# Normalisation, splitting and rounding of eleven routing tiles moved from the router into the readout

## The reference

```python
x = x + tanh(g_xattn[0]) * readout(layernorm(x), ctx_2048, mask)   # softmax(x ctx^T / sqrt(512)) ctx
x = x + tanh(g_ffn[0]) * ffn(layernorm(x), router_w, wg, wu, wd)
...
logits = einsum('bsh,eh->bse', x, router_w)         # 8 experts
idx = argmax(logits, -1)
xq = clip(round(x * s), -128, 127) / s, s = 127 / max|x|   # each row, before each expert's ternary matrix
```

## Time and profile before

| what | us |
|---|---|
| median of 3 runs | 1711.72 |
| lowest, highest | 1705.13, 1719.22 |
| the profiled execution, its own time | 1718.61 |
| its span | 1716.9 |
| TensorE busy in the span | 1453.8 (85%) |
| VectorE busy | 1252.0 (73%) |
| ScalarE busy | 970.3 (57%) |
| GpSimd busy | 418.7 (24%) |

### The profile page before, as it was taken

One profiled execution on the slowest core, in us unless ns is written; L12 is line 12 of the kernel. 1 busy time (PEld: TensorE's weight loads), 2 busy tenths in 40 slices (PEclk: granted clock), 3 DMA queues, 4 the chain that ended last, 5 costly groups with the idle time before them and its releaser, 6 DMA issues. The chain is left out here.

```text
span 1716.9 us, 24336 instructions
## 1 busy us (share of the span) xinstructions
PE 1453.8 (85%) x8479; PEld 835.5 (49%) x8551; DVE 1252.0 (73%) x1525; ACT 970.3 (57%) x1440; POOL 418.7 (24%) x328
## 2 busy tenths in 40 slices
PE   4998996999822795779999999999968599999996
PEld 3454443555422443314555555555533466666663
DVE  4787855655484696669999999999787676665651
ACT  5787733344243684415766677676833676665651
POOL 0122200000053006204555656555740000000000
PEclk9999998999955896868999999999989799999998
DMA  6788760000064439310423324244254586666640
GB/s 226 220 271 296 236 210 26 0 0 0 1 243 167 141 119 228 88 49 15 103 71 88 83 68 107 70 102 132 73 167 178 181 291 216 220 213 224 225 144 25
DMA packets 145824, 236.74 MB, mean 138 GB/s; under 512 B 11324, under 2 KB 61503, under 8 KB 144584
## 3 DMA queue, kind: packets, MB, share of 16 engines
q1 hardware_dynamic: 140232, 210.39, 39.8%
q0 software_dynamic: 5504, 25.20, 4.0%
HBM read 169.48 MB, written 59.59 MB: 133 GB/s over the span
## 5 line engine op out<-in xcount | busy, mean ns | idle before, releaser
L1687 ACT ACTIVATE t_e<-t_psE 128x512 f32<-128x512 f32 x512 | 304.6, 597 | 139.6 <-PE t_psE L1812 131.3
L1725 DVE TENSOR_REDUCE t_nmax<-t_psM 128x1 f32<-128x1024 f32 x256 | 301.7, 1211 | 15.1 <-PE t_psM L1793 15.1
L1644 POOL TENSOR_TENSOR t_low<-t_e 128x1024 bf16<-128x1024 f32 x128 | 249.9, 1954 | 201.2 <-ACT t_e L1687 179.4
L1823 PE MATMUL t_psO<-t_e,vst 128*96 128x512 bf16 x512 | 201.1, 393 | 2.5 <-POOL t_low L1644 2.5
L1812 PE MATMUL t_psE<-qst,kst 99*128 99x512 bf16 x512 | 195.9, 384 | 0.1
L1823 PE MATMUL t_psO<-t_low,vst 128*96 128x512 bf16 x512 | 193.6, 378 | 0.0
L1793 PE MATMUL t_psM<-kst,qst 96*128 96x512 bf16 x512 | 165.1, 406 | 30.8 <-DVE t_nmax L1725 25.5
L1733 DVE TENSOR_TENSOR t_low<-t_e 128x1024 bf16<-128x1024 f32 x128 | 175.4, 1371 | 17.8 <-ACT t_e L1687 17.3
L2281 PE MATMUL e_psG<-prebob,e_w1p 128*128 (+1 forms) x1536 | 174.4, 277 | 11.6 <-DVE e_hT L2225 6.9
L2281 PEld LDWEIGHTS e_psG<-prebob,e_w1p 128*128 128x128 bf16 x1536 | 152.2, 99 | 34.1 <-issue 8.1
L2296 PE MATMUL e_psO<-e_w2p,e_hT 128*128 128x512 bf16 x752 | 164.9, 379 | 0.8
(11 more groups left out here) (235 smaller groups left out, 2286.5 us busy)
## 6 DMA issues: line engine op xcount, KB each, us to landing
piece<-in_L_ffn_w SPq DMA_DIRECT2D x32, 1024.0 KB, 13.9
xres<-in_L_ffn_w SPq DMA_DIRECT2D x32, 1024.0 KB, 14.6
wT<-ternary POOLq DMA_DIRECT2D x8, 1536.0 KB, 21.4
kst<-keys SPq DMA_DIRECT2D x96, 128.0 KB, 4.6
mixed<-t_ost SPq DMA_DIRECT2D x64, 192.0 KB
c_rows<-in_ctx SPq DMA_DIRECT2D x8, 1024.0 KB, 10.4
xres<-in_L_ffn_wg SPq DMA_DIRECT2D x8, 1024.0 KB, 7.8
xres<-in_L_ffn_wu SPq DMA_DIRECT2D x8, 1024.0 KB, 7.5
```

Source lines behind the costliest of these rows:

```text
L1644: nc.gpsimd.tensor_tensor(low[:, slot(h, u), :, :], e32[:, slot(h, u), :, :], upper(h, u), ALU.subtract).then_inc(lo_pool, 1)
L1687: nc.scalar.activation(e32[:, slot(h, u), i, :], psE[:, i, :], ACT.Exp, scale=SC).then_inc(expd, 1)
L1725: nc.vector.tensor_reduce(nmax[:, h // G % 2, h % G, u:u + 1], banks_of(place_of_max(b, m)).rearrange("p a t -> p (a t)"), AX_X, ALU.max, ...
L1823: last = nc.tensor.matmul(psO[0:VW, h % 2, :], vst[:, g, 2 * u + i, :].rearrange("p (w h) -> p h w", h=G)[:, h % G, :], part[:, i, :], sta ...
```

## The change

Tiles 0 to 10 (ROUTED_EARLY = 11) are normalised, split and rounded in the readout, by a function `route(r)` at the end of step r + 5 on VectorE and ScalarE. The router does this only for tiles 11 to 15 and transposes the others as they are. So that results can stay where they are written, the memory of the later stages (`late_flat`) is reserved from the start, and the first 22 of the 32 tiles of `ctxN` lie in it; `route` writes its pairs and integers over rows of `ctxN` whose batch is done, and uses rows of `ctxT` of the first batch as scratch. bn_aggr of a tile follows its bn_stats directly, GpSimd computes rstd for three batches within the readout (`rrstd`), and the hardware loops of the readout are written straight out on all engines. The second array `disp_late` holds the integers of the last two tiles, whose scales need an instruction of their own. On TensorE x_transposes(0) moves ahead of the router weights' transposes, and on ScalarE the copy of tile 0 ahead of the router weights' copy.

```diff
 # readout, ScalarE
+                def route(r):
+                    act.wait_ge(rnormed, r + 1)
+                    act.wait_ge(readout, r // QD * QD + 6)
+                    nc.scalar.copy(xpairs[:, r, 0, :], rxn[r % 2]).then_inc(rhi_done, 1)
+                    act.wait_ge(rq_ready, r + 1)
+                    nc.scalar.activation(disp[:, r, 0:D], rq32, ACT.Copy, bias=-MAGIC).then_inc(rq_cast, 1)
...
                     if further_x:
                         x_copy(t + 3, 1 - par)
+                    if 0 <= t - 5 < ROUTED_EARLY:
+                        route(t - 5)
...
-                with act.Fori(0, NT // 2 - 2) as i:
-                    step(2 * i, 0, 2, True)
-                    step(2 * i + 1, 1, 2, True)
+                for t in range(NT - 4):
+                    step(t, t % 2, 2, True)
 # readout, VectorE
                     nc.vector.bn_stats(stats[:, bass.ds(t, 1), :].rearrange("p o d -> p (o d)"), row).then_inc(stats_ready, 1)
+                    dve.wait_ge(stats_ready, t + 1)
+                    nc.vector.bn_aggr(moments[:, t, :], stats[:, t, :]).then_inc(moments_ready, 1)
+
+                def route(r):
+                    v, xn_r = nc.vector, rxn[r % 2]
+                    dve.wait_ge(rrstd_ready, r // QD + 1)
+                    if r >= 2:
+                        dve.wait_ge(rlo_done, r - 1)
+                    v.tensor_scalar(xn_r, xres[:, r, :], moments[:, r, 0:1], rrstd[:, r:r + 1],
+                                    ALU.subtract, ALU.mult).then_inc(rnormed, 1)
+                    dve.wait_ge(rnormed, r + 1)
+                    v.tensor_reduce(peak[:, r:r + 1], xn_r, AX_X, ALU.max, apply_absolute_value=True).then_inc(peaked, 1)
+                    dve.wait_ge(peaked, r + 1)
+                    v.tensor_scalar(amax[:, r:r + 1], peak[:, r:r + 1], EPS, 1.0 / 127.0, ALU.max, ALU.mult).then_inc(amax_ready, 1)
+                    dve.wait_ge(amax_ready, r + 1)
+                    v.reciprocal(invs[:, r:r + 1], amax[:, r:r + 1]).then_inc(invs_ready, 1)
+                    dve.wait_ge(invs_ready, r + 1)
+                    if r >= 1:
+                        dve.wait_ge(rq_cast, r)
+                    v.tensor_scalar(rq32, xn_r, invs[:, r:r + 1], MAGIC, ALU.mult, ALU.add).then_inc(rq_ready, 1)
+                    dve.wait_ge(rhi_done, r + 1)
+                    v.tensor_tensor(xpairs[:, r, 1, :], xn_r, xpairs[:, r, 0, :], ALU.subtract).then_inc(rlo_done, 1)
...
                         p_lo(t + 1, 1 - par)
+                    if 0 <= t - 5 < ROUTED_EARLY:
+                        route(t - 5)
...
-                dve.wait_ge(stats_ready, NT)
-                for t in range(NT):
-                    nc.vector.bn_aggr(moments[:, t, :], stats[:, t, :]).then_inc(moments_ready, 1)
 # router, ScalarE
-                for t in range(QD):
-                    high(t)
                 act.wait_ge(router_loaded, 16)
                 nc.scalar.copy(rpair[:, 0, :], rows[:, :]).then_inc(router_hi, 1)
+                x_copy(0)
                 act.wait_ge(router_xposed, 1)
                 nc.scalar.copy(rT[:, :, :], psR[:, :, 0:E]).then_inc(router_ready, 1)
-                for t in range(NT):
+                for t in range(1, NT):
                     x_copy(t)
-                    if t + QD < NT:
-                        high(t + QD)
-                    integers(t)
+                    if t - 1 + ROUTED_EARLY < NT:
+                        high(t - 1 + ROUTED_EARLY)
+                        integers(t - 1 + ROUTED_EARLY)
 # router, VectorE (route(t) here: normalise, peak, scale, reciprocal, multiply of one tile)
+                dve.wait_ge(consts, RSTD)
+                for t in range(ROUTED_EARLY, NT):
+                    route(t)
+                    if t > ROUTED_EARLY:
+                        low(t - 1)
+                low(NT - 1)
 # router, TensorE
                 def x_transposes(t):
-                    pe.wait_ge(x_lo, t + 1)
+                    if t >= ROUTED_EARLY:
+                        pe.wait_ge(x_lo, t - ROUTED_EARLY + 1)
```

More of the change, by code:

```diff
@@ L396, in _, with routed_views, readout_phase @@
                         gemm(q, n)
-def readout_phase(nc, sem, mask, gates, ident, ctxN, ctxT, xres, moments):
+ROUTED_EARLY, ROUTED_SHARED = 11, 14
+RW = 2 * D + DW
+def routed_views(flat):
+    v = flat[:, 0:ROUTED_SHARED * RW].rearrange("p (t w) -> p t w", w=RW)
+    return v[:, :, 0:2 * D].rearrange("p t (r d) -> p t r d", r=2), v[:, :, 2 * D:]
+def readout_phase(nc, sem, mask, gates, ident, ctxN, ctxT, xres, moments, amax, routed):
     SC = float(D) ** -0.5
@@ L459, in _ @@
                 nc.gpsimd.tensor_tensor(rstd[:, :], veps[:, :], half[:, :], ALU.pow).then_inc(rstd_ready, 1)
+                for b in range(B - 1):
+                    q = slice(b * QD, (b + 1) * QD)
+                    pool.wait_ge(moments_ready, (b + 1) * QD)
+                    nc.gpsimd.tensor_scalar(rveps[:, q], moments[:, q, 1], EPS, None, ALU.add).then_inc(rveps_ready, 1)
+                    pool.wait_ge(rveps_ready, b + 1)
+                    nc.gpsimd.tensor_tensor(rrstd[:, q], rveps[:, q], half[:, q], ALU.pow).then_inc(rrstd_ready, 1)
             @block.scalar
@@ L590, in _ @@
                 step(0, 0, False, True, True)
-                step(1, 1, True, True, True)
-                with dve.Fori(1, NT // 2 - 2) as i:
-                    step(2 * i, 0, True, True, True)
-                    step(2 * i + 1, 1, True, True, True)
+                for t in range(1, NT - 4):
+                    step(t, t % 2, True, True, True)
                 step(NT - 4, 0, True, False, True)
@@ L661, in _ @@
                 scores(1, 1, 0)
-                with pe.Fori(0, NT // 2 - 2) as i:
-                    step(2 * i, 0, True, True)
-                    step(2 * i + 1, 1, True, True)
+                for t in range(NT - 4):
+                    step(t, t % 2, True, True)
                 step(NT - 4, 0, True, True)
@@ L757, in _ @@
                     done(nc.gpsimd.memset(z, 0.0))
-                done(nc.gpsimd.memset(disp[:, :, D + 2:DW], 0.0))
+                done(nc.gpsimd.memset(disps[:, :, D + 2:DW], 0.0))
+                done(nc.gpsimd.memset(disp_late[:, :, D + 2:DW], 0.0))
                 for e in range(E):
@@ L815, in _ @@
                 v = nc.vector
-                def normalise(t):
-                    if t >= 2 * QD:
-                        dve.wait_ge(q_ready, t - 2 * QD + 1)
-                    v.tensor_scalar(xn[:, t % (2 * QD), :], xres[:, t, :], moments[:, t, 0:1], rstd[:, t:t + 1],
-                                    ALU.subtract, ALU.mult).then_inc(normed, 1)
-                def scale(g):
-                    for t in range(g * QD, (g + 1) * QD):
-                        dve.wait_ge(normed, t + 1)
-                        v.tensor_reduce(peak[:, t:t + 1], xn[:, t % (2 * QD), :], AX_X, ALU.max, apply_absolute_value=True).then_inc(amax_raw, 1)
-                    q = slice(g * QD, (g + 1) * QD)
-                    dve.wait_ge(amax_raw, (g + 1) * QD)
-                    v.tensor_scalar(amax[:, q], peak[:, q], EPS, 1.0 / 127.0, ALU.max, ALU.mult).then_inc(amax_ready, 1)
-                    dve.wait_ge(amax_ready, g + 1)
-                    v.reciprocal(invs[:, q], amax[:, q]).then_inc(invs_ready, 1)
@@ L843, in _, with route @@
-                dve.wait_ge(consts, RSTD)
-                for t in range(QD):
-                    normalise(t)
+                def route(t):
+                    n = t - ROUTED_EARLY
+                    if n >= 3:
+                        dve.wait_ge(x_lo, n - 2)
+                        dve.wait_ge(q_ready, n - 2)
+                    v.tensor_scalar(xn[:, t % 3, :], xres[:, t, :], moments[:, t, 0:1], rstd[:, t:t + 1],
+                                    ALU.subtract, ALU.mult).then_inc(normed, 1)
+                    dve.wait_ge(normed, n + 1)
+                    v.tensor_reduce(peak[:, t:t + 1], xn[:, t % 3, :], AX_X, ALU.max, apply_absolute_value=True).then_inc(amax_raw, 1)
+                    dve.wait_ge(amax_raw, n + 1)
+                    v.tensor_scalar(amax[:, t:t + 1], peak[:, t:t + 1], EPS, 1.0 / 127.0, ALU.max, ALU.mult).then_inc(amax_ready, 1)
+                    dve.wait_ge(amax_ready, n + 1)
+                    v.reciprocal(invs[:, t:t + 1], amax[:, t:t + 1]).then_inc(invs_ready, 1)
+                    dve.wait_ge(invs_ready, n + 1)
+                    if n >= 2:
+                        dve.wait_ge(q_cast, n - 1)
+                    v.tensor_scalar(q32[:, t % 2, :], xn[:, t % 3, :], invs[:, t:t + 1], MAGIC, ALU.mult, ALU.add).then_inc(q_ready, 1)
```

110 lines of the change are left out of this document (59 added, 51 removed).

## The result

| | before | changed |
|---|---|---|
| median of 14 runs, us | 1710.20 | 1700.02 |
| lowest, highest | 1705.13, 1719.22 | 1694.53, 1701.76 |
| profiled execution, own time (span) | 1718.61 (1716.9) | 1700.02 (1698.3) |

The ratio is 0.9929, 95% interval 0.9916 to 0.9942: 12.1 us faster, which is also the distance of the two means; the medians of the table lie 10.2 us apart. The forecast was 12.2. A second measurement beside other runs of the kernel before gave 0.9946 (0.9926 to 0.9967), 9.2 us, so the two together say 9 to 12.

What follows compares the result with a forecast made beforehand. TensorE was taken to pace the readout and a serial chain to set the router. 13.4 us gained in the router less 1.2 lost in the readout, 12.2 off the median 1711.72, gave 1699.5 us; range 1689 to 1710.

Steps and rivals of the forecast that it cites:

- Readout pace: Readout steps: VectorE's chain becomes 11.96 us against TensorE's 11.70; a cover of 1.4 us leaves TensorE 0.4 us lost.
- Rival (1): Readout: it becomes VectorE's, with a chain of 12.7 us; 6 to 10 us lost, time 1705 to 1709; chance 0.15.
- rival (2): Readout: VectorE and ScalarE hand the route back and forth; chain 13.95 us, 23 us lost, time 1721; chance 0.05.
- Step 14: Readout's end: no cover there, so the route delays the copy and read(15); 1.6 to 3.0 us lost, 2.2 taken.
- bn_aggr: Readout's end: one of the sixteen bn_aggr is left there, which gives back 1.0 us.
- Router: Router: logits' maximum 27.5 us after M, the memset's end, against 41.1; ten late copies 1.43 us apart; 13.4 us gained.
- rival (5): Router: copies 6 to 15 run at ScalarE's 1.04 to 1.2 us; 2 to 3.5 us more gain, 1697; chance 0.05.
- The memset: Router's head: GpSimd's memset blocks VectorE's new first normalisation as before; the old one stood for 10.3 us.
- Rival (4): Router's head: memset doesn't hold the first normalisation; 1.6 us more gain (1697.9), or 1689 if nothing is held; chance 0.08.
- Scatters: Router's end: scatters and everything behind unchanged in length; 0 charged for meeting the weights' fetch, 2 us as a bound.
- rival (3): Router's end: scatters wait for the weights' fetch to land; 2 to 3 us less gain, 1702; chance 0.07.
- The sum: Whole kernel: 13.4 us gained in the router less 1.2 lost in the readout, 12.2 us faster, 1699.5; forecast's chance 0.60.

Runs made afterwards that it cites:

- e6: The changed kernel with each route in the readout taking its peak twice, first into a spare tile: 1709.40 us, 0.9976 of the kernel before.
- e1: The kernel before with the readout's loops written straight out and bn_aggr inside the steps, no routing work moved: 1709.68 us, 0.9994 of the kernel before.
- e2: The changed kernel with nine tiles moved into the readout instead of eleven: 1699.38 us, 0.9936 of the kernel before.
- e4: The changed kernel with the route of tile 9 moved from step 14 to step 15, behind its update: 1695.58 us, 0.9902 of the kernel before.
- e9: e7 with idle matmuls on TensorE, eight at the router's head and two a tile: 1686.22 us, 0.9842 of the kernel before.
- e5: The changed kernel with a memset of a quarter of the size, stored four times: 1696.08 us, 0.9895 of the kernel before.
- e8: e1 with the changed kernel's memory layout (late_flat holding part of ctxN), no tile moved: 1712.84 us, 0.9981 of the kernel before.
- e7: The changed kernel with the quarter memset, tile 9's route in step 15 and ScalarE's copies interleaved with casts: 1689.86 us, 0.9863 of the kernel before.

## Why the prediction was right

**Readout pace: right.** The chain was put at 11.96 us and is 11.73. It never overran, so the 0.4 us charged to TensorE wasn't due. Rival (1) and rival (2) needed chains of 12.7 and 13.1; e6 shows that rival (1)'s mechanism is real: with 0.6 us a step more it costs time from the third routed step on. In the changed kernel VectorE is busy 78%, under the 80 to 90 that I had named. e1 shows that the loops themselves had cost TensorE nothing.

**Step 14: right in kind, a little small.** The route of tile 9 delays read(15), forecast 2.2 with the 0.4. p_transposes(15) comes 0.2 later (161.49 against 161.26 us behind p_transposes(1); e1, without any route, has 161.48, so this is not the route's), read(15) starts another 1.4 behind it, and it runs 1.0 longer, the cost that I named as a bound (up to 3.6) and took as none. That is 2.7; less the 1.0 of the bn_aggr the readout lost 1.7 against 1.2. e2 leaves both last routes out and wins these 2.7 back; e4 moves the one of tile 9 and wins 2.9 in the stretch, in part by the clock.

**bn_aggr: right.** Forecast 1.0, measured 1.0 behind read(15) in e1.

**Router: right in mechanism, one term mis-sized.** Two copies before M, a stand of 7.8 us (forecast some 9), integers of tile 15 at M + 12.95 (M + 12.9), then ten copies. These were the mis-sized term: 1.43 us apart in the forecast, 13.9 in all; measured 11.0. I took the distance from two copies that had a cast between them, and held TensorE to be as slow once the cast is gone. But e9 shows that this distance was ScalarE's copy and cast, and the earlier trace rows had said so: ScalarE was busy 1.00 of 1.00 us there (528 to 529), TensorE 0.48. Without the cast the first four distances average 1.2 us with TensorE at its lower level, and the last six copies, during which it comes back to the upper one, are 1.0 apart. That is rival (5), at the 2 to 3.5 us which it named: 16.7 gained instead of 13.4. By the prediction's own list this was a sign of being wrong, as was the mixture's other length; the maximum of the logits, which should have come 27.5 us after M, came after 24.5. The router weights' low half ended before the memset began (477.88), at no cost.

**The memset: right.** It holds the new normalisation as it held the old. Rival (4) falls in both its forms, and e5 shows cause and size. The Trainium skill (SBUF — State Buffer, "Who interferes with whom") gives the port pair to whoever issues first. If a record's start is taken for the issue, the traces disagree: they show VectorE starting 20 ns ahead and held all the same, here and with the small memset.

**Scatters: right.** From the first of them to the first load it is 24.35 us; rival (3), which wanted 2 to 3 us more there, falls.

**The sum: partly luck.** The stretch gained 15.0 us where the steps gave 12.2, and the timing shows 12.1 and 9.2. The faster copies (3 us) were missed, and so was what came back later: 1.4 to 1.6 us in the mixture, shown above. What was missed on one side nearly cancelled what was missed on the other, and that is luck. The forecast time of 1699.5 had luck of its own: it stood on a median of three, 1711.72, where fourteen runs gave 1710.20. The rest stays open. In all nine runs with tiles moved the timed gain, by the ratio, is 1 to 6 us smaller than the stretch's; in e1 the two agree. From the first load to the last store the three profiles of before took 1134 to 1141 us, and the eight with eleven tiles 1139 to 1145, on the mean 5.5 longer. But the query stage (first to last record of its matmuls, 93 to 94 us or 95 to 96), the attention's output (the same, 69 or 72) and the experts (to the last store, 347 to 348 in before, 344 in e1, 347 to 351 with eleven tiles) jump between profiles of one kernel, and none of these was tried by itself. The layout by itself can account for 1.4 us at most (e8).

## What to carry to other kernels

Work moved under the engine that sets the pace is free until the other engine's serial chain is as long as the step, not until that engine is busy all the time. VectorE went from 60 to 78% and its chain was already full (11.73 us in a step of 11.70); of 0.6 us more a step, each full step paid 0.6 once 1.4 us of cover were used. The last step of a pipeline has no cover, so a moved piece belongs behind the instruction for which the last step waits (2.9 us here, a part of it by the clock). And when finished work becomes available early, the in-order queue of its consumer decides what it is worth: with the copies in front of the first blocked instruction the same change gained 7.2 us more.

## What the runs showed of the hardware

- A GpSimd memset of 10.34 us held a VectorE normalisation that was recorded as starting 20 to 30 ns before it and ended 0.28 us behind it, in all eleven profiles with this memset; beside one of 2.59 us (e5, e7, e9) it again ended 0.28 us behind.
- TensorE's clock changed the length of matmuls that nobody had edited: the last four products of the mixture took 1.03 us in six profiles and 1.7 to 1.9 in eight, and read(15) took 5.34, 6.7, 7.03 or 8.07 for the same 24 matmuls, 5.34 and 7.03 behind the same gap of 1.93 us.
- In the changed kernel the granted clock rose from 0.50 to 1.00 between 507 and 508 us, with TensorE busy 8.35 of 10 us in short matmuls (500 to 510); in e7 it stayed at 0.50 although TensorE was busy 9.47 of 10 us (485 to 495). What tells the two apart was not settled.
- ScalarE's copy of a 128x1024 tile and a cast of 128x512 behind it took 1.43 us together, with TensorE at either level (1.42 in the earlier trace rows at 0.50, 1.43 in e9 at 1.00).
